# A fused attention and butterfly feed-forward kernel: one head's first loads spread over four chunks, negated keys made in the preparation, a lead of 19 tiles for 21

## The reference

```python
xn = layernorm(x)
qkv = (xn @ W_qkv + b_qkv).reshape(B, D, 3, 16, 16).transpose(2, 0, 3, 1, 4)      # 16 heads of 16 dimensions
scores = softmax(einsum('bhip,bhjp->bhij', q, k), axis=-1)
out = einsum('bhij,bhjp->bhip', scores, v).reshape(B, D, N)
h = butterfly(xn @ W_exp + b_exp, up_weights)
h = butterfly(gelu(h + up_bias), down_weights)
x = x + out + (h @ W_con + b_con + down_bias)
```

## Time and profile before

| | us |
|---|---|
| median of 3 runs | 5677.05 |
| lowest, highest | 5672.97, 5677.72 |
| the profiled execution, its own time | 5674.86 |
| its span, first to last instruction | 5673.1 |

### The profile page before, as it was taken

One profiled execution on the slowest core, in us unless ns is written; L12 is line 12 of the kernel. 1 busy time (PEld: TensorE's weight loads), 2 busy tenths in 40 slices (PEclk: granted clock), 3 DMA queues, 4 the chain that ended last, 5 costly groups with the idle time before them and its releaser, 6 DMA issues. The chain is left out here.

```text
span 5673.1 us, 97332 instructions
## 1 busy us (share of the span) xinstructions
PE 5605.1 (99%) x35880; PEld 2613.5 (46%) x35880; DVE 4884.6 (86%) x9104; ACT 4977.2 (88%) x9651; POOL 524.8 (9%) x482
## 2 busy tenths in 40 slices
PE   8799999999999999999999999999999999999999
PEld 5444444444444444444444444444444444444698
DVE  6689999999999999999999999999999999996233
ACT  3489999999999999999999999999999999999544
POOL 2245564000000000000000000000000000000000
PEclk9889999999999999999999999999999999999999
DMA  8611111000000000000000000000000000000111
GB/s 288 200 43 43 50 54 42 21 21 19 14 16 21 21 21 21 15 21 21 21 18 14 16 21 21 21 20 16 21 21 21 17 12 20 21 21 2 34 44 41
DMA packets 232761, 197.02 MB, mean 35 GB/s; under 512 B 171752, under 2 KB 192616, under 8 KB 220520
## 3 DMA queue, kind: packets, MB, share of 16 engines
q1 hardware_dynamic: 228848, 168.00, 10.4%
q0 software_dynamic: 3456, 23.07, 1.4%
HBM read 128.07 MB, written 60.82 MB: 33 GB/s over the span
## 5 line engine op out<-in xcount | busy, mean ns | idle before, releaser
L646 ACT ACTIVATE probs<-psum 128x512 f32<-128x512 f32 x8192 | 4222.6, 608 | 294.8 <-PE psum L843 292.8
L708 DVE TENSOR_REDUCE maxima<-psum 128x1 f32<-128x512 f32 x6036 | 3966.7, 686 | 364.7 <-PE psum L821 255.6
L821 PE MATMUL psum<-k_rows,q_rows 48*128 48x512 f32 x7042 | 2494.3, 455 | 0.6 <-ACT spill L670 0.6
L857 PE MATMUL psum<-probs,v_cols 128*32 128x512 f32 x16384 | 2184.7, 605 | 0.5
L843 PE MATMUL psum<-q_rows,k_rows 50*128 50x512 f32 x8192 | 2061.2, 424 | 0.0
L821 PEld LDWEIGHTS psum<-k_rows,q_rows 48*128 48x128 f32 x7042 | 1176.6, 184 | 1248.8 <-DVE maxima L704 809.6
L843 PEld LDWEIGHTS psum<-q_rows,k_rows 50*128 50x128 f32 x8192 | 1266.5, 186 | 135.0 <-ACT probs L646 44.5
L704 DVE CUSTOM_DVE_ANT_0 merged<-psum,spill 128x512 bf16<-128x512 f32 x1006 | 684.8, 681 | 2.7 <-issue 1.9
L670 ACT ACTIVATE spill<-psum 128x512 f32<-128x512 f32 x1006 | 601.0, 597 | 23.9 <-PE psum L821 23.6
L857 PEld LDWEIGHTS psum<-probs,v_cols 128*32 128x32 f32 x16384 | 323.3, 108 | 622.0 <-issue 325.8
L821 PEld LDWEIGHTS psum<-k_diff,q_rows 48*128 48x128 f32 x1006 | 184.6, 183 | 843.0 <-DVE maxima L708 787.7
(11 more groups left out here) (94 smaller groups left out, 2067.0 us busy)
## 6 DMA issues: line engine op xcount, KB each, us to landing
q_rows<-q_parts SPq DMA_DIRECT2D x128, 256.0 KB
q_parts<-parts SPq DMA_DIRECT2D x32, 512.0 KB, 6.0
k_parts<-parts SPq DMA_DIRECT2D x32, 512.0 KB, 3.7
k_rows<-k_parts SPq DMA_DIRECT2D x64, 256.0 KB
q_rows<-q_parts SPq DMA_DIRECT2D x128, 128.0 KB
planes<-in_up_planes POOLq DMA_DIRECT2D x10, 1024.0 KB, 11.3
planes<-in_down_planes POOLq DMA_DIRECT2D x10, 1024.0 KB, 5.4
y<-in_x SPq DMA_DIRECT2D x16, 512.0 KB, 6.0
```

Source lines behind the costliest of these rows:

```text
L646: nc.scalar.activation(probs[:, 2 * (u % 2) + half, BANK * g:BANK * g + BANK], ps_s[:, r % 4, :], ACT.Exp).then_inc(s_exp, 1)
L708: nc.vector.tensor_reduce(largest, region(use), axis=AX_X, op=ALU.max).then_inc(s_region_free, 1)
L821: nc.tensor.matmul(region(use_of[n, j]), q_rows[m % 4][lower:lower + ROWS, P * t:P * t + P], keys[lower:lower + ROWS, :], start=True, stop ...
L857: last = nc.tensor.matmul(ps_o[VW * g:VW * g + VW, :], v_cols[:, KT * (head % 2) + UNITS * half + at, :], probs[:, 2 * (u % 2) + half, BAN ...
```

## The change

The loads of the first head are no longer issued together at chunk 12. They follow the stores of chunks 9, 10, 11 and 12: the keys of one half, the keys of the other with the difference, the queries of one half, the queries of the other. The negated keys get a buffer of their own in the preparation, `k_minus`, and ACT fills it in chunk 15, between the high parts and the cast for the key difference. `TURN_TILE` is 1 and `AHEAD` 19, so `PAIRED` is 17. The paired stage's buffers move to `probs[:, 1]` and the upper half of `probs[:, 0]`, and ACT waits before the first exponential until the last paired reduction is done. `planes` and `fold` (POOL's) are placed behind the preparation's memory.

```diff
-    TURN_TILE = 2
-    AHEAD = QT + 5
+    TURN_TILE = 1
+    AHEAD = QT + 3
...
+        k_minus = sb("k_minus", [P, 2, BANK], F32R, until=prepare)
...
-        def load_q(sp, head, half, slot):
+        def load_q(sp, head, half, slot, halves=(0, 1)):
             rows = bass.ds(HD * head, HD)
-            for lower in (0, HALF_P):
+            for lower in (HALF_P * n for n in halves):
                 for first, part, copies in ((0, 0, 2), (2, 1, 1)):
...
-        def load_k(sp, head, slot):
+        def load_k(sp, head, slot, halves=(0, 1), difference=True):
             rows = bass.ds(HD * head, HD)
-            for half in range(2):
+            for half in halves:
...
-            for first, count in ((0, 2), (2, 1)):
+            for first, count in ((0, 2), (2, 1)) if difference else ():
...
                 def step(c, i, p, before, left):
-                    if left == 4:
-                        for m in range(2 * KD):
-                            sp.wait_ge(s_parts_out[m], 16 * (CHUNKS // B))
-                        sp.wait_ge(s_diff_out, 16 * KD)
-                        load_k(sp, 0, 0)
-                        load_q(sp, 0, 0, 0)
                     if left > 4:
...
                     sp.dma_start(dst, v_sb[:, HEADS * p:HEADS * p + HEADS, :]).then_inc(s_v_out[p], 16)
+                    if c == IN_ROW + 1:
+                        for m in range(2 * KD):
+                            sp.wait_ge(s_parts_out[m], 16 * IN_ROW)
+                        sp.wait_ge(s_diff_out, 16 * KD)
+                    if c in (IN_ROW + 1, IN_ROW + 2):
+                        load_k(sp, 0, 0, halves=(c - IN_ROW - 1,), difference=c == IN_ROW + 2)
+                    if c in (IN_ROW + 3, IN_ROW + 4):
+                        load_q(sp, 0, 0, 0, halves=(c - IN_ROW - 3,))
...
+                    if left == 1:
+                        act.wait_ge(s_k[0], 16 * K_LOADS)
+                        for lower in (0, HALF_P):
+                            keys = k_rows[0][lower:lower + ROWS, :].rearrange("p (c two k) -> p c two k", two=2, k=BANK)
+                            nc.scalar.activation(k_minus[lower:lower + ROWS, :, :], keys[:, :, 1, :], ACT.Copy, scale=-1.0)\
+                              .then_inc(s_minus, 1)
                     b, of_row = c // IN_ROW, c % IN_ROW
                     if of_row == DIFF_TO:
...
-                def minus_k():
-                    wait_for_stores(act)
-                    act.wait_ge(s_k[0], 16 * K_LOADS)
-                    for lower in (0, HALF_P):
...
-                minus_k()
                 for n in range(PAIRED):
                     for i in range(PAIRS_OF_TILE):
                         rectify_pair(n, i)
                 for n in range(PAIRED, AHEAD):
                     rectify(n)
                 act.wait_ge(s_ones_in, 16 * 4)
+                act.wait_ge(s_region_free, vector_uses[use_of[PAIRED - 1, "second", PAIRS_OF_TILE - 1]])
                 for r in range(QG):
                     exp(0, r)
...
-                        if 0 < m <= SUPER and t == 1:
+                        if 0 < m <= SUPER and t == 0:
                             if j == 1:
                                 negate(m - 1)
...
-                    for what, keys, second in (("apart", k_rows[0], 0), ("apart", k_rows[1], 1), ("second", k_rows[0], 1)):
+                    for what, keys, second in (("apart", k_rows[0], 0), ("apart", k_minus, 1), ("second", k_rows[0], 1)):
```

More of the change, by code:

```diff
@@ L107, in attention_and_butterfly_ffn @@
         w_down_t = sb("w_down_t", [P, KD, HID])
-        planes = sb("planes", [P, 2, 4, PAIRS], until=before_ffn)
-        fold = sb("fold", [P, 3, PAIRS], until=before_ffn)
         q_rows = [sb("q_rows0", [P, QB], F32R, until=before_ffn)]
@@ L163, in attention_and_butterfly_ffn @@
         s_w = sem("weights_loaded")
+        s_minus = sem("minus_k_made")
         s_ident = sem("ident_made")
@@ L423, in attention_and_butterfly_ffn @@
         probs = sb("probs", [P, 4, QG * BANK], until=before_ffn)
+        planes = sb("planes", [P, 2, 4, PAIRS], until=before_ffn)
+        fold = sb("fold", [P, 3, PAIRS], until=before_ffn)
         v_cols = sb("v_cols", [P, 2 * KT, VW], until=before_ffn)
@@ L520, in _ @@
                 wait_for_stores(pool)
-                nc.gpsimd.memset(probs[0:MAX_PARTS, 0, :], 1.0).then_inc(s_ones, 1)
+                nc.gpsimd.memset(probs[0:MAX_PARTS, 2, :], 1.0).then_inc(s_ones, 1)
                 ones = Chain(pool, s_set)
@@ L612, in _ @@
                         dst = k_rows[slot][lower + ROWS:lower + ROWS + MAX_PARTS, :].bitcast(F32)
-                        sp.dma_start(dst, probs[0:MAX_PARTS, 0, :]).then_inc(s_ones_in, 16)
+                        sp.dma_start(dst, probs[0:MAX_PARTS, 2, :]).then_inc(s_ones_in, 16)
                 sp.wait_ge(s_set, 2)
@@ L647, in exp @@
                                          ps_s[:, r % 4, :], ACT.Exp).then_inc(s_exp, 1)
-                def minus_k():
-                    wait_for_stores(act)
-                    act.wait_ge(s_k[0], 16 * K_LOADS)
-                    for lower in (0, HALF_P):
-                        src, dst = (k[lower:lower + ROWS, :].rearrange("p (c two k) -> p c two k", two=2, k=BANK)[:, :, 1, :]
-                                    for k in k_rows)
-                        nc.scalar.activation(dst, src, ACT.Copy, scale=-1.0).then_inc(s_minus, 1)
                 def rectify_pair(n, i):
@@ L714, in reduce_pair @@
                     dve.wait_ge(s_region, vector_uses[use])
-                    largest_of_pair = probs[:, 2, BANK * (nth % QG):BANK * (nth % QG) + BANK // 2].bitcast(BF16)
-                    nc.vector.tensor_tensor_reduce(largest_of_pair, region(use), probs[:, 3, BANK * (nth % QG):BANK * (nth % QG) + BANK],
+                    at = 2 * BANK + BANK // 2 * (nth % QG)
+                    largest_of_pair = probs[:, 0, at:at + BANK // 2].bitcast(BF16)
+                    nc.vector.tensor_tensor_reduce(largest_of_pair, region(use), probs[:, 1, BANK * (nth % QG):BANK * (nth % QG) + BANK],
                                                    1.0, LOWEST, ALU.add, ALU.max,
@@ L796, in pairs @@
                             lower, at = HALF_P * half, BANK * (2 * two + second)
-                            if keys is not k_rows[1]:
+                            rows = slice(lower, lower + ROWS)
+                            operand = k_minus[rows, two, :] if keys is k_minus else keys[rows, at:at + BANK]
+                            if keys is not k_minus:
                                 free_region(use_of[n, what, pair])
                             last = nc.tensor.matmul(region(use_of[n, what, pair]), q_rows[m][lower:lower + ROWS, P * t:P * t + P],
-                                                    keys[lower:lower + ROWS, at:at + BANK],
-                                                    start=keys is not k_rows[1], stop=what == "second" or keys is k_rows[1])
+                                                    operand, start=keys is not k_minus, stop=what == "second" or keys is k_minus)
                             if what == "second":
                                 last.then_inc(s_region, 1)
-                            elif keys is k_rows[1]:
+                            elif keys is k_minus:
                                 last.then_inc(s_diff_ps, 1)
```

3 lines of the change are left out of this document (1 added, 2 removed).

## The result

| | before | after |
|---|---|---|
| median, us | 5676.88 (6 runs) | 5654.91 (6 runs) |
| lowest, highest | 5672.97, 5677.72 | 5647.46, 5657.56 |
| profiled execution, span | 5674.86, 5673.1 | 5647.46, 5645.7 |

The ratio is 0.9963, 95% interval 0.9953 to 0.9973: the changed kernel is 22.0 us faster. The prediction said 16.75 us less, which is 5658.1 for the profiled execution and 5660.5 for the median, with a range from 5651 to 5671. The profiled execution after is the fastest of its six, so its own time is not set against 5658.1; the stages are compared instead.

The account below looks back on a forecast made before the run. It saw PE busy 99% overall, with the preparation held up by loads on two DMA engines; -6.0 - 5.25 - 7.0 + 1.5 = -16.75 us gave 5658.1 for the profiled execution, 5660.5 for the median, range 5651 to 5671.

Parts of the forecast that it names:

- What bounds the preparation: Chunk 12's stretch: the first loads clog two DMA engines while fourteen stand idle, 20.8 us summed against 20.7 in the trace.
- Part 1: Preparation, chunks 10 to 13: spreading the first loads lets spare time take up part of the clog, -6.0 us.
- Part 2: Start of attention: negation in chunk 15 saves 6.6 us of PE's wait, delays the block by 1.35; -5.25 us.
- Part 3: Before the main loop: lead of 19 saves a paired and a single-piece tile, -7.0 us; two units with pieces, +1.5.
- The new lead of one unit: Every superblock: turned maxima lead the first score by one unit, yet are in place about 1.5 us early; 0.
- Clock: First two units: PE's wait remains, so the same two run at 1.2 GHz; 0, bounds -5.9 and +3.3 us.
- Sum: Whole kernel: -6.0 - 5.25 - 7.0 + 1.5 = -16.75 us.
- Rival 1: Preparation: the spread hides the loads altogether, -20.7 us there, time 5646; chance 0.08.
- Rival 2: Preparation: the clog comes back whole in four pieces, saving 0 there, time 5666; chance 0.17.
- Rival 4: First units: two fewer or one more run at 1.2 GHz, time 5654.5 or 5664; chance 0.08.
- Rival 5: Every superblock: maxima land too late for the first score, making the kernel slower, about 5803 or 5692; chance 0.05.

Follow-up runs that it names:

- Experiment 4: The changed kernel with every 32-row transfer in load_q and load_k issued as two of 16 rows, in all superblocks: 5639.98 us, ratio 0.9942.
- experiment 1: The changed kernel with only the spread undone, all ten first loads again before chunk 12's stores: 5660.47 us, ratio 0.9978.
- experiment 10: The changed kernel with transfers of 16 rows, but all first loads (fifteen issues) before chunk 12's stores: 5653.42 us, ratio 0.9958.
- experiment 2: The changed kernel with only the negation moved back to the start of attention, after all stores: 5660.16 us, ratio 0.9979.
- experiment 3: The changed kernel with TURN_TILE = 2 and AHEAD = QT + 5 (lead of 21) again: 5659.71 us, ratio 0.9978.
- experiments 6: The changed kernel with two extra 16 KB copies to DRAM on SP before each superblock's maxima are placed: 5649.52 us, ratio 0.9964.
- experiment 8: The changed kernel with unused 48-row matmuls, eight before the turned maxima and one behind each piece of tiles 17 and 18: 5653.88 us, ratio 0.9971.
- experiment 5: The changed kernel without an edit, run again beside the kernel before in the second group: 5652.08 us, ratio 0.9967.
- experiment 11: The changed kernel with 16-row transfers, plus unused 128-row matmuls, six before the turned maxima, one behind each piece: 5657.06 us, ratio 0.9964.
- experiment 7: The changed kernel with four extra 16 KB copies to DRAM on SP before each superblock's maxima are placed: 5674.48 us, ratio 1.0006.

## Why the prediction was right

*What bounds the preparation*: right in the main. Experiment 4 takes the clog away by the shape of the loads alone, and experiment 1 puts it back. That the sum on two engines came within 0.1 us of the clog (20.8 against 20.7) was in part luck: with the shape mended and the place kept, experiment 10, the stretch falls by 12.8 us and 7.8 are left.

*Part 1, -6.0 us*: measured -7.3. Chunks 10 to 13 were forecast at 15.4, 17.6, 14.6, 14.6 and took 16.22, 17.59, 14.26, 14.46; the excess of 14.2 was 14.6. The step that was off is the chunk that follows: it took 11.54 us before and was forecast at 12.0, but took 10.03. The four long stretches hold 57 + 47 + 33 + 46 = 183 matmuls, where four chunks have 4 x 41 = 164: PE had done 19 of the next ones while ACT waited, and chunk 14 had 25 left. That alone does not shorten a chunk: before, chunk 13 had 5 left and took 11.54 us, because PE stood idle for 18.96 us until DVE's low part came. In experiments 2, 3, 6 and 8, where PE's clock stays at 1.00 in chunk 14, it takes 8.7 us, so that part 1 would be another 1.3 us larger.

*Part 2, -5.25 us*: measured -5.45 from the first high part of chunk 15 to the first pair, and 6.7 us by experiment 2. The 6.6 us of waiting went as said, and the preset came 12.31 us after chunk 15's first high part, for a forecast of 12.2. The delay of the casts does reach DVE: its difference operations start 8.53 us after chunk 15's first high part in experiment 3 and 7.14 in experiment 2, 1.39 later. But the step from there to the block's end, which the prediction took in full, costs 1.1 us with the loads at chunk 12 (experiment 1), and between nothing and 0.5 with them spread (experiment 2), because SP's queue, still busy with earlier stores, ends the block at nearly the same time anyhow.

*Part 3, -7.0 + 1.5 us*: the paired tile and the tile of single pieces are right: from turned maxima to first exponential -4.55, against 4.58. The paired stage gained 4.36 in place of 2.44. PE's wait for the maxima, which the prediction kept at 3.19 us, was 0.83. It goes with the lead: 3.19 and 2.59 us in the two traces with a lead of 21 (before, experiment 3), 0.63 to 1.39 in the nine with 19 in which nothing fills it. With 21 PE does the product of the difference before the wait, with 19 in the middle of it, so that a shorter wait is not all time gained: from the first pair to the turned maxima experiment 3 takes 47.16 us and experiment 5 44.42, 2.7 less, close to the 2.44. The rest of the 4.36 lies between executions: the kernel before took 48.00 and the first trace of the changed one 43.64, and DVE's cast of 16 columns there 1.26 and 0.17 us, against 0.67 and 0.76 in experiments 3 and 5. Why it varies was not tried.

*The new lead of one unit, 0*: right. The room is 1.5 us, as the prediction had it.

*Clock, 0*: measured -2.15. The two units take 7.48 and 6.19 us, where they took 7.48 and 8.16; this lies between the two bounds of the prediction. It is not the change's doing as far as the runs show: experiments 1, 2 and 4, all with the lead of 19, have 7.48 and 8.16 again. That the wait decides over it, as the prediction assumed, is refuted by experiments 8 and 11.

*Sum*: -16.75 against -22.0 and -18.3 in two groups, each with an interval of some 6 us to either side. The three terms that were short (1.3, 1.9, 2.15) all fell to the side of faster, and the order of the terms was right. That they did is luck for the clock and for most of the paired stage, which other executions do not repeat; the 18.3 us of the second group are the nearer test. (5658.1 and the 2.2 us between the two times make 5660.3, not the 5660.5 that the prediction gives.) Rival 1 is out: the excess was 14.6, not 0. Rival 2 also, since it was not 20. Rival 4, the clock, came about in small: 2 us in the two traces of the changed kernel. Rival 5 is out by experiments 6 and 7.

## What to carry to other kernels

A load that keeps few DMA engines busy while the mean share is low is a matter of shape first and of place second: look at the share in the stretch of the clog, find the transfers whose source has a slowest dimension of 2, and split them (12.8 us here) before they are moved. Where a transfer is made later or its consumer earlier, use up the room on purpose, as the copies aside did, and learn how many microseconds are left. Undo each part of a change by itself and read its price in the trace from a point that both kernels share, because a place counted from the start of the span also holds what the stages before it gained or lost: 6 us are plain there, while the times of single runs differ by 10.

## What the runs showed of the hardware

- PE's clock stood at 1.2 GHz (0.50) for 27 us (265.3 to 292.6, experiment 8) and from 259.4 to 286.7 (experiment 11) while PE was busy for nearly all of the time. Keeping PE at work did not raise it.
- In the kernel before it stood at 0.50 from 269.8 to 276.4 us with PE busy for all of the 6.60 us.
- One issue of 256 KB on two engines and one of 128 KB behind it held SP's queue for 8.28 to 8.57 us in three places, and for 3.67 in a fourth. Six of 128 KB held it for 5.60 (keys) and 2.73 (queries) in experiment 10.
- The share of the DMA engines was 1.02 at 205 GB/s (experiment 10, chunk 12) and 1.07 at 301 GB/s (experiment 4, chunk 10): a full share does not tell how much is moved.
- The same kernel's superblock took 78.06 us in one execution and 78.15 in another, 0.1%, with the same instructions; over 63 superblocks this is 5.7 us and more than any term of the prediction was off by.
- Two transfers of 16 KB, issued one after the other on SP, were in place 2.93 us after the first issue at the earliest, and 3.06 at the latest, in 56 superblocks of experiment 7.
